# Moving two operands of TensorE by 32 bytes: where the gated output's and the GELU rows' parts start in SBUF

## What is computed

```python
# block 1, with x normalised over its 256 features
xz = x @ w_in                              # 256 -> 2 * 512
xp, z = split(xz)
xc = silu(causal_conv4(xp) + conv_b)       # depthwise, 4 taps
h = h * 0.9 + 0.1 * (xc_t @ w_B)           # scan over the tokens, 16 states
y = (h @ w_C) * silu(z)
x = x + y @ w_out                          # 512 -> 256

# block 2, with x normalised again
idx = top2(x[:, 0] @ Wr + br)              # two experts of 8 per sequence, by its first token
h = gelu(x @ W1[idx] + b1[idx])            # 256 -> 256, for each of the two
x = x + (h @ W2[idx] + b2[idx]).sum() / 2
```

## Time and profile before

| | |
|---|---|
| median of three runs | 507.56 us |
| the profiled execution's own time | 506.41 us |
| its span, first to last instruction | 504.6 us |
| granted TensorE clock, mean | 1.000 of full speed |
| TensorE matmuls busy | 499.1 us, 99% of the span, 3026 matmuls |
| weight loads busy | 438.7 us, 87% |
| VectorE / ScalarE / GpSimd busy | 451.8 / 400.6 / 348.7 us (90 / 79 / 69%) |

### The profile page before, as it was taken

How to read it: one execution, slowest core, us unless ns; L and a number is a source line. 1 busy time by engine, 2 the same in 40 slices (tenths; PEclk the granted TensorE clock), 3 DMA queues, 4 the chain that set the end, 5 groups by cost and what they waited for, 6 DMA issues and landing times.

```text
span 504.6 us, 9913 instructions
## 1 busy us (share of the span) xinstructions
PE 499.1 (99%) x3026; PEld 438.7 (87%) x3026; DVE 451.8 (90%) x896; ACT 400.6 (79%) x692; POOL 348.7 (69%) x390
## 2 busy tenths in 40 slices
PE   7999999999999999999999999999999999999997
PEld 7888799888888888888888888888888888888997
DVE  6999899889998899989999899998999989996773
ACT  4986958878869789697887969879797888969454
POOL 4959587659593796928969197782977649773391
PEclk9999999999999999999999999999999999999999
DMA  8940105435251442606235170432604334130102
GB/s 258 292 185 7 37 1 168 125 127 168 73 183 40 162 129 83 208 15 196 81 125 166 42 224 25 166 125 86 205 36 138 117 125 126 52 116 1 42 2 84
DMA packets 53379, 57.28 MB, mean 114 GB/s; under 512 B 8682, under 2 KB 49642, under 8 KB 53226
## 3 DMA queue, kind: packets, MB, share of 16 engines
q1 hardware_dynamic: 51498, 56.67, 34.3%
q10 hardware_dynamic: 1856, 0.31, 0.3%
HBM read 35.46 MB, written 21.50 MB: 113 GB/s over the span
## 4 chain that ended last, share of the span: by engine, by line
PE 97%; DVE 1%; DMA 1%; issue 0%; DVEq 0%
PE blk L1294 16%; PE blk L1295 16%; PE blk L1301 16%; PE tok L1415 12%; PE tok L1417 11%; PE tok L1416 11%; PE turn L1466 3%; PE turn L1469 3%; PE blk L1490 3%; PE turn L1242 1%; PE tok L1294 1%; PE tok L1301 1%; PE tok L1295 1%; DMA x_mid<-in_L_attn_x 1%; DVE stats_t L917 0%; DVE normed L934 0%
## 5 line engine op out<-in xcount | busy, mean ns | idle before, releaser
L992 DVE SCALAR_TENSOR_TENSOR conv<-blk,tap_w,conv 128x512 f32<-128x512 f32 x192 | 130.1, 741 | 7.1 <-ACT conv L683 6.0
L488 POOL TENSOR_TENSOR y_lo<-gate,y_hi 128x512 fp32r<-128x512 f32 x57 | 72.2, 1299 | 35.1 <-ACT y_hi L611 35.1
L1294 PE MATMUL blk<-xn_hi,w_in_hi 128*128 128x512 f32 x228 | 89.4, 392 | 0.0
L1295 PE MATMUL blk<-xn_hi,w_in_lo 128*128 128x512 f32 x228 | 89.0, 391 | 0.0
L453 POOL TENSOR_TENSOR xc_lo<-conv,xc_hi 128x512 fp32r<-128x512 f32 x60 | 73.4, 1242 | 7.5 <-ACT xc_hi L611 7.3
L1415 PE MATMUL tok<-w_out_hi,y_hi 128*128 128x256 f32 x256 | 72.2, 282 | 0.0
L1417 PE MATMUL tok<-w_out_hi,y_lo 128*128 128x256 f32 x256 | 70.8, 277 | 0.0
L1416 PE MATMUL tok<-w_out_lo,y_hi 128*128 128x256 f32 x256 | 70.8, 276 | 0.0
L1301 PE MATMUL blk<-xn_lo,w_in_hi 128*128 128x512 f32 x228 | 70.3, 389 | 0.0
L1415 PE MATMUL tok<-w_hi,hid_hi 128*128 128x256 f32 x248 | 70.3, 283 | 0.0
L683 ACT ACTIVATE conv<-blk,tap_b,tap_w 128x512 f32<-128x512 f32 x64 | 49.1, 778 | 25.1 <-PE blk L1301 22.0
(11 more groups left out here) (189 smaller groups left out, 1318.2 us busy)
## 6 DMA issues: line engine op xcount, KB each, us to landing
spill<-normed SPq DMA_DIRECT2D x25, 512.0 KB, 2.8
normed<-spill SPq DMA_DIRECT2D x100, 128.0 KB, 2.8
out<-x_mid SPq DMA_DIRECT2D x30, 256.0 KB, 2.2
x_mid<-in_L_attn_x SPq DMA_DIRECT2D x29, 256.0 KB, 2.7
x_in<-in_L_attn_x SPq DMA_DIRECT2D x14, 512.0 KB, 4.4
w_all<-in_L_ffn_W SPq DMA_DIRECT2D x2, 2048.0 KB, 11.3
b_all<-in_L_ffn_b SPq DMA_DIRECT2D x1, 1024.0 KB, 13.4
gate<-in_L_attn_w_in SPq DMA_DIRECT2D x2, 256.0 KB, 4.8
```

The source lines that it names most:

```text
L488: nc.gpsimd.tensor_tensor(y_lo[:, j, :], gate_of(o, j), y_hi[:, j, :].bitcast(F32), ALU.subtract).then_inc(y_lo_set, 1)
L992: nc.vector.scalar_tensor_tensor(cols, blk[j][:], tap_w[:, j, t:t + 1], cols, ALU.mult, ALU.add).then_inc(tap_added, 1)
L1294: mm(dst, whi(k), his(k), start=(k == 0), stop=False)
L1295: ins = mm(dst, wlo(k), his(k), start=False, stop=False)
```

## The change

The unused 16 numbers ahead of `y_hi` become 8, and 16 unused numbers are put between `y_lo` and `hid_hi`. `y_hi` and `y_lo` then start 32 bytes behind a multiple of 512, `hid_hi` and `hid_lo` 96 bytes behind one. No instruction, wait or transfer is added, taken out or moved; the addresses of these four tensors are all that differs.

```diff
@@ -96,8 +96,9 @@
         w1_hi, w1_lo = sb("w1_hi", [P, TOP_K, KD * D], F32R), sb("w1_lo", [P, TOP_K, KD * D], F32R)
         b_mix = sb("b_mix", [P, JD, P], F32R)
         c_mix = sb("c_mix", [P, DI], F32R)
-        behind_columns = sb("behind_columns", [P, 16])
+        in_front_of_y = sb("in_front_of_y", [P, 8])
         y_hi, y_lo = sb("y_hi", [P, JD, CH], F32R), sb("y_lo", [P, JD, CH], F32R)
+        in_front_of_hid = sb("in_front_of_hid", [P, 16])
         hid_hi, hid_lo = sb("hid_hi", [P, JF, CH], F32R), sb("hid_lo", [P, JF, CH], F32R)
```

## The result

The changed kernel takes 512.45 us (median of four runs, 512.24 to 512.98) against 507.42 us: 1.0101 times the time before, 95% interval 1.0084 to 1.0119. It is slower by 5.0 us, above the range of the prediction. Of the rivals it is B with both operands (513.0 us).

The account below looks back on a forecast made before the run. The prediction took the distance between TensorE's matmul starts as the bound. Every part of the change was priced at 0, so the forecast stayed at the runs' median, 507.5 us, with a range of 505.9 to 511.0.

Parts of the forecast that it names:

- B with both operands: y at 32 and hid at 96 both settle at the middle pace: +5.5 us, 513.0 us; chance 0.10 with anything worse.
- What bounds the kernel: Whole kernel: TensorE's matmuls with hardly a hole, 97% of the chain; distance between starts costs time, paced restarts stay.
- The three paces: TensorE's 256-column matmuls start 113.3 ns apart (quick), about 118 (middle) or 120 (slow, opening's w_in at offset 0).
- The step that failed: 768 y matmuls at 32 and 768 hid matmuls at 96 were assumed to keep the paces of 64: cost 0.
- The two terms put at 0: Output projection's y matmuls and second expert product's hid matmuls, each 0, bounded by +5.1 and -3.4 us before deductions.
- the prediction's bounds of 109 and 120 ns: Distances for y and hid matmuls: 109 ns from the transposes, 120 ns from the opening's matmuls at offset 0.
- Rival B: New offsets lose the quick pace after restarts: y alone 510.6 us, hid alone 509.9; one operand 0.22, both or worse 0.10.
- one operand: Only y or only hid settles at the middle pace: +3.1 us (510.6) or +2.4 us (509.9); chance 0.22.
- Rival A: hid at 96 turns quick behind `state_out`: -1.0 us, perhaps -0.6 more from halved slips, say 506.2 us; chance 0.24.
- Rival C: A better offset brings y and hid matmuls to 109 ns: -6.8 us, 500.7 us; chance 0.02.
- What fits an offset of 0 is what 64 does not fit: TensorE's weight load and moving operand read as two streams whose fit depends on stationary byte offset and how they met.
- The Trainium skill's rule: TensorE's moving-operand and weight-load ports are independent, so no offset matters: sum exactly 0; the prediction doubted it was complete.

## Why the prediction was wrong

- *What bounds the kernel*: right. Clock, chain and waits are unchanged, and the distance between starts is all that moved.
- *The three paces, and that y's and hid's matmuls alone are touched*: right; 5.67 of 5.84 us stand in them.
- *The step that failed*: "I take the quick 113.3, the row of the same form and the nearest in bytes: 0", and the same for hid. Nearness in bytes meant nothing. 64 is not a place on a slope: of the differences tried within 32 bytes of it (32, 48, 80, 96) none has the quick pace. The two terms put at 0 measured +3.40 us (y, 118.2 ns) and +2.27 us (hid, 117.5 ns behind a restart), between the prediction's bounds of 109 and 120 ns.
- *Rival B's price* was right: 4.4 ns for each y matmul, 768 x 4.4 - 0.3 = 3.1 against 3.40; hid 2.4 against 2.27; both 513.0 against 512.45. That it fits so well is in part luck: B priced 64's own middle pace, which goes in even steps of 117 to 119 ns (118 in the mean), while y at 32 goes in uneven ones of 115 to 123 that happen to average 118.2. Its chances were not right. The prediction took "one operand" (0.22) as likelier than "both" (0.10), as if the two were independent draws. They hang in large part on one question, whether 64 is special or only one of many good offsets, and so the cases tend to stand and fall together; the range, cut above y alone, left out the likeliest way to lose.
- *Rival A*: nothing of it at 96 (118.6 behind `state_out`). Its premise, that `state_out` at offset 0 leaves TensorE in a state that 64 can't leave, is borne out by c_mix at 64.
- *Rival C*: no 12 y or hid matmuls in a row below 113.3 ns at any offset.
- *"What fits an offset of 0 is what 64 does not fit"* was read rightly, but taken for the 256-column matmuls alone. With all operands at 64 it turned out to hold both ways: 512 columns settle at 226.7 with a difference of 0 and at 233.3 with 64, 256 columns at 120 with 0 and at 113.3 (or 117.8) with 64.
- *The Trainium skill's rule* that the two read ports of TensorE wait for nobody (the Trainium skill, SBUF — State Buffer, Who interferes with whom) would have made the change free. The runs disagree by 4 to 7 ns a matmul, with nothing changed but addresses; it describes the ports, and the trace shows that it doesn't describe the pace.

What stays open is why. That two streams meet at all is the prediction's reading, and no run shows where in SBUF or TensorE they would, or why a difference of 64 or 192 bytes would let them pass. Only that the difference counts was shown, and that for offsets from a multiple of 512 bytes; other distances between the tensors were not varied by themselves.

## What to carry to other kernels

In this kernel, where TensorE is the bound and each matmul loads new weights, the byte offset of the loaded operand against the moving one was worth 4 to 6% of these matmuls' time. In one like it, read the distance between their starts in the timeline, not their busy time, and compare it with the best distance of the same form. Try offsets one by one for each shape (of 0 and 64, what was better for 256 columns was worse for 512), and look at the pace behind each change of operands too, since the same address ran at either of two paces depending on what came before. And where two bounds depend on the same unknown, don't multiply their chances.

## What the runs showed that was not expected

- Two paces for one address: with a difference of 64 bytes, runs of 24 matmuls last 2.72 or 2.827 us, and in the steps of the loop a run nearly always keeps the one that it has after its first four or five matmuls.
- A restart that costs TensorE 81 ns (194 - 113) pays: without it the kernel before is 2.0 us slower, although it then waits 30 times less.
- The sign doesn't matter at 64, the one difference tried both ways: y at 0 with w_out at 64 is as quick as y at 64 with w_out at 0.
- 32, 48, 80, 96 and 128 bytes mostly run in irregular cycles of 112 to 127 ns from one start to the next, with means of 117 to 121; 0 and 256 in a steady 120 behind a restart, and 96 in some steps too (y in two steps of the kernel with y at 96).
